# Four-image non-local block on one core: statistics, tile order of the last block, first exponentials, shared maxima and the final stage rebuilt

## The reference, cut to what matters

```
xn = group_norm(x, 32 groups)                      # per image
f = xn^T xn                                        # 4096 x 4096, symmetric
attn = softmax(f, axis=-1)
y = (g_w xn + g_b) attn^T                          # 128 x 4096
wy = W_w y + W_b                                   # 256 x 4096
wy = (wy - mean) * rsqrt(var + 1e-5) * gamma + beta  # over b, h, w
out = x + xn + wy
```

## Time and profile before

| | |
|---|---|
| median of 3 runs | 2142.32 us |
| the profiled execution's own time | 2144.3 us |
| its span | 2142.6 us |
| mean granted TensorE clock | 0.991 |
| busy: TensorE, VectorE, ScalarE, GpSimd | 96%, 73%, 51%, 38% |
| HBM read, written | 157.55 MB, 140.51 MB |

### The profile page before, as it was taken

One profiled execution on the slowest core, in us unless ns is written; L12 is line 12 of the kernel. 1 busy time (PEld: TensorE's weight loads), 2 busy tenths in 40 slices (PEclk: granted clock), 3 DMA queues, 4 the chain that ended last, 5 costly groups with the idle time before them and its releaser, 6 DMA issues.

```text
span 2142.6 us, 32272 instructions
## 1 busy us (share of the span) xinstructions
PE 2049.1 (96%) x9348; PEld 1459.3 (68%) x9348; DVE 1574.8 (73%) x3123; ACT 1086.5 (51%) x2234; POOL 810.9 (38%) x623
## 2 busy tenths in 40 slices
PE   5999999999999999999999999999999999999988
PEld 4787777656588777666668777765658777766433
DVE  5776777777776777787767677777777777777656
ACT  4344554455435445547454455445544554555645
POOL 4011233458501113448631123346850211345750
PEclk9999999999999999999999999999999999999999
DMA  3222233546412333455522223354641133347877
GB/s 125 116 96 87 94 117 113 191 142 201 157 66 74 114 120 107 164 176 156 185 88 97 88 94 117 113 191 142 200 158 77 58 118 113 99 133 235 306 284 294
DMA packets 107254, 300.29 MB, mean 140 GB/s; under 512 B 11456, under 2 KB 11840, under 8 KB 93248
## 3 DMA queue, kind: packets, MB, share of 16 engines
q1 hardware_dynamic: 107072, 298.11, 40.7%
HBM read 157.55 MB, written 140.51 MB: 139 GB/s over the span
## 4 chain that ended last, share of the span: by engine, by line
PE 76%; issue 7%; POOL 5%; DVE 5%; ACT 4%; DMA 2%; SPq 0%; DVEq 0%; ACTq 0%; POOLq 0%
PE bank L1258 14%; PE bank L1181 11%; PE bank L1183 11%; PE bank L1182 11%; PE bank L1234 8%; PE bank L1262 4%; PE bank L1264 4%; PE bank L1263 4%; PE bank L1411 2%; ACT ring L793 2%; POOL fy_c L726 2%; PE bank L1328 2%; POOL fy_d L726 2%; DMA fy_c<-spill 1%; DVE plo L1012 1%
## 5 line engine op out<-in xcount | busy, mean ns | idle before, releaser
L819 ACT CAST phi<-bank 128x512 fp32r<-128x512 f32 x480 | 282.2, 588 | 759.9 <-PE bank L1234 758.6
L976 DVE TENSOR_SCALAR_CACHE_REDUCE ring<-bank 128x512 f32<-128x512 f32 x560 | 385.6, 690 | 293.9 <-PE bank L1183 230.4
L1181 PE MATMUL bank<-xh 128*128 128x512 f32 (+3 forms) x1152 | 514.1, 446 | 6.1 <-POOL xl L699 5.9
L1012 DVE TENSOR_TENSOR plo<-bank,phi 128x512 fp32r<-128x512 f32 x480 | 329.2, 687 | 150.1 <-ACT phi L819 104.0
L1183 PE MATMUL bank<-xh,xl 128*128 128x512 f32 (+3 forms) x1152 | 436.1, 379 | 0.0
L1182 PE MATMUL bank<-xl,xh 128*128 128x512 f32 (+3 forms) x1152 | 433.7, 376 | 0.0
L793 ACT ACTIVATE ring<-ring,nmax 128x512 f32<-128x512 f32 x464 | 334.7, 723 | 37.0 <-DVE nmax L1003 37.0
L726 POOL TENSOR_TENSOR fy_d<-fy_d,maxrow 128x512 f32<-128x512 f32 x188 | 244.8, 1305 | 271.2 <-DMA fy_d<-spill 271.1
L1234 PEld LDWEIGHTS bank<-ident,ring 128*128 128x128 f32 x1856 | 223.5, 141 | 157.8 <-issue 84.7
L726 POOL TENSOR_TENSOR fy_c<-fy_c,maxrow 128x512 f32<-128x512 f32 x200 | 259.7, 1301 | 174.7 <-DMA fy_c<-spill 174.4
L1234 PE MATMUL bank<-ident,ring 128*128 128x128 f32 x1856 | 283.9, 276 | 21.6 <-DVE plo L1012 15.4
(11 more groups left out here) (138 smaller groups left out, 2770.5 us busy)
## 6 DMA issues: line engine op xcount, KB each, us to landing
spill<-ring SPq DMA_DIRECT2D x108, 1024.0 KB, 4.3
fy_c<-spill SPq DMA_DIRECT2D x200, 256.0 KB, 4.1
fy_d<-spill SPq DMA_DIRECT2D x188, 256.0 KB, 4.1
ring<-x_dram SPq DMA_DIRECT2D x42, 512.0 KB, 4.8
lbuf<-spill SPq DMA_DIRECT2D x60, 256.0 KB, 3.6
yd<-yn SPq DMA_DIRECT2D x24, 256.0 KB, 2.9
out_dram<-ring SPq DMA_DIRECT2D x10, 512.0 KB, 3.6
fx_a<-x_dram SPq DMA_DIRECT2D x8, 512.0 KB, 6.6
```

What stands on the lines that cost most here:

```text
L819: nc.scalar.copy(phi[:, HI_BUF[n], :], whole(p)).then_inc(hi_made, 1)
L976: last = nc.vector.tensor_scalar(slot_tile(u, t), src, 1.0, None, ALU.mult, ALU.max, accum_out=rowm[:, t, c:c + 1])
L1012: nc.vector.tensor_tensor(plo[:, n % LOS, :], whole(p), phi[:, HI_BUF[n], :].bitcast(F32), ALU.subtract).then_inc(lo_made, 1)
L1181: nc.tensor.matmul(dst, xh[:, k, rows], xh[:, k, cols], start=(k == 0), stop=False)
```

## The change

1. **Statistics**: STATS_STEP goes from 148, 149, 150, 151, 157, 164, 166, 167 to 142, 144, 149, 152, 157, 159, 165, 169; the group stages from 170, 172, 174, 175 to 172, 174, 176, 177; the normalization of x 2 steps later; the next image's first products at steps 184 to 238 (182 to 239 before).
2. **Block 7**: right, then 28 left, then 3 right tiles. Before: R R L R L R, then left tiles to the end.
3. **First exponentials**: chunk 0 of block 0 at steps -12, -11, -9, -8 (-7 to -4 before), chunk 1 at -3, -3, -2, -1, the last at step 20 (24 before).
4. **Maxima shared**: of the last image's blocks 6 and 7, 15 of 56 left tiles (every third from the fifth loaded one on, VSUBS) get their maxima subtracted by VectorE (`subtract_row`), 5 steps ahead of their step; GpSimd skips them.
5. **Final loads**: spread up to step 244. The first y goes from step 215 to 222; x of image 3 is loaded at 251 (piece 2) where before it was at 235 (piece 1).
6. **Final stage**: 30 half pieces (one k, 2 banks) and 4 quarter pieces in place of 16 pieces. The products of the first 4 (8 matmuls) are copied by ScalarE out of PSUM into `keep`, `lbuf`, `maxrow` and `lsb` ahead of `bn_ready`, and TensorE goes on with the next 4. `phi` and `plo` now lie where `keep` comes to lie later.

```diff
-    if j == NB - 1:
-        at = [0.04 * q for q in range(nr)]
-    elif j == NB - 2:
+    if j >= NB - 2:
         at = [0, 0.9, 0.95, 1]
...
-FIRST_EXP = -7
+FIRST_EXP = -12
...
+            if j == 0:
+                q = T * c + t
+                step = FIRST_EXP + 3 * q // 2 if q < T else (q - T) * 6 // 7 - 3
+            at[j, c, t] = max(step, min(merged, j * TPB - LAG - 1))
...
-STATS_STEP = [COLS_STEP[5] + 2 + c if c < 4 else X_STEP[c] + (12 if c == 5 else 6) for c in range(NB)]
+STATS_STEP = [X_STEP[c] + lag for c, lag in enumerate((6, 7, 9, 11, 6, 7, 5, 8))]
...
-NEXT_AT, NEXT_TO = XN_STEP[0] + 5, TILES - 17
+NEXT_AT, NEXT_TO = XN_STEP[0] + 5, TILES - 18
...
+VSUBS = [w for j in (NB - 2, NB - 1) for w in [w for w in LEFT_OF[j] if LEFT_BUF[w] is not None][VSUB_FROM::3]]
...
+UNITS = [(b, q, k, 0, FW // W) for b, q in PIECES[:-1] for k in range(K)] + \
+    [(*PIECES[-1], k, h, 1) for k in range(K) for h in range(FW // W)]
+KEPT = 4
...
+        def kept(u, h):
+
+            n = FW // W * u + h
+            if n < HIS + LOS:
+                return keep[:, n, :]
+            return (lbuf[:, 0, :], maxrow[:, :], lsb[:, :])[n - HIS - LOS]
...
+                    if not more and w in VSUBS:
+                        continue
...
                 w = LEFT_NO[p]
-                act.wait_ge(left_sub, b * NLEFT + w + 1)
+                if isinstance(b, int) and b == B - 1 and w in VSUBS:
+                    act.wait_ge(left_sub_v, VSUBS.index(w) + 1)
+                else:
+                    act.wait_ge(left_sub, pool_subs(b, w) + 1)
...
+            act.wait_ge(tile_used, B * TILES)
+            act.wait_ge(left_added, B * NLEFT)
+            for u in range(KEPT):
+                act.wait_ge(fin_wy, u + 1)
+                for h in range(FW // W):
+                    last = nc.scalar.copy(kept(u, h), unit_bank(u)[:, h, :])
+                last.then_inc(fin_kept, 1)
+
             act.wait_ge(bn_ready, 1)
...
+            def subtract_row(b, w):
+
+                mine = LOADS[LEFT_BUF[w]]
+                dve.wait_ge(loaded[LEFT_BUF[w]], b * (16 * len(mine)) + 16 * (mine.index(w) + 1))
+                dve.wait_ge(maxrow_made, b * (NB - 1) + tile(LEFT[w])[0])
+                nc.vector.tensor_tensor(left_at(w), left_at(w), maxrow[:, :], ALU.subtract).then_inc(left_sub_v, 1)
...
+                if not more and p + VSUB_LEAD in LEFT_NO and LEFT_NO[p + VSUB_LEAD] in VSUBS:
+                    subtract_row(b, LEFT_NO[p + VSUB_LEAD])
...
+                if u < KEPT:
+                    dve.wait_ge(fin_kept, u + 1)
+                    for a in range(n):
+                        last = nc.vector.scalar_tensor_tensor(out=px[:, a, :], in0=kept(u, a), scalar=bnp[:, 1, k:k + 1],
+                                                              in1=px[:, a, :], op0=ALU.mult, op1=ALU.add)
...
+                        elif u < 4 + KEPT:
+                            pe.wait_ge(fin_kept, u - 3)
                         else:
-                            pe.wait_ge(fin_added, f - 1)
+                            pe.wait_ge(fin_added, u - 3)
```

More of the change, by code:

```diff
@@ L245 @@
 X_STEP = [last_use(LAST_IN_SLOT[X_SLOT + c // 2]) + 1 + c % 2 for c in range(NB)]
-STATS_STEP = [COLS_STEP[5] + 2 + c if c < 4 else X_STEP[c] + (12 if c == 5 else 6) for c in range(NB)]
-assert all(s > X_STEP[c] + 5 for c, s in enumerate(STATS_STEP)) and STATS_STEP == sorted(STATS_STEP)
+STATS_STEP = [X_STEP[c] + lag for c, lag in enumerate((6, 7, 9, 11, 6, 7, 5, 8))]
+assert all(s >= X_STEP[c] + 5 for c, s in enumerate(STATS_STEP)) and STATS_STEP == sorted(STATS_STEP)
 GROUP_AT = STATS_STEP[-1] + 3
@@ L401, in nonlocal_block @@
             gl = scoped("gl", [P, NB, T, CI])
+            phi = scoped("phi", [P, HIS, W])
+            plo = scoped("plo", [P, LOS, W])
         fx_a = sb("fx_a", [P, K, N])
@@ L560, in left_at, with pool_subs, unit_bank, unit_x @@
             return (fy_c, fy_d)[h][:, row * W:(row + 1) * W]
+        def pool_subs(b, w):
+            n = b * NLEFT + w
+            return n - sum(v < w for v in VSUBS) if isinstance(b, int) and b == B - 1 else n
+        def kept(u, h):
[3 more added lines that the diff above has]
+            return (lbuf[:, 0, :], maxrow[:, :], lsb[:, :])[n - HIS - LOS]
+        def unit_bank(u):
+            return bank[:, 2 * (u % 4):2 * (u % 4) + UNITS[u][4], :]
+        def unit_x(u):
+            b, q, k, h, n = UNITS[u]
+            return fx(b, k, q)[:, h:h + n, :]
         def y_home(b, j):
@@ L677, in _ @@
                 load_final(False, 2, q)
[L678 to L685, removed]
-            sp.wait_ge(fin_out, 16 * K * B * FQ)
+            for q in range(FQ):
+                if LATE_X.get(q, TILES) >= TILES:
+                    load_final(True, 3, q)
+            for u, (b, q, k, h, n) in enumerate(UNITS):
+                cols = slice(q * FW + h * W, q * FW + (h + n) * W)
+                sp.wait_ge(fin_added, u + 1)
+                sp.dma_start(outd[b, :, k, cols].rearrange("p (a w) -> p a w", w=W), unit_x(u)).then_inc(fin_out, 16)
+            sp.wait_ge(fin_out, 16 * len(UNITS))
         @block.gpsimd
@@ L800, in take_maxrow @@
                 if j > 1:
-                    act.wait_ge(left_sub, b * NLEFT + LEFT_OF[j][0])
+                    act.wait_ge(left_sub, pool_subs(b, LEFT_OF[j][0]))
+                if isinstance(b, int) and b == B - 1 and VSUBS[0] < LEFT_OF[j][0]:
+                    act.wait_ge(left_sub_v, sum(v < LEFT_OF[j][0] for v in VSUBS))
                 nc.scalar.copy(maxrow[:, :], sps).then_inc(maxrow_made, 1)
@@ L1145, in _ @@
             last.then_inc(bn_ready, 1)
-            for f, (b, q) in enumerate(PIECES):
-                dve.wait_ge(fin_scaled, f + 1)
-                dve.wait_ge(fin_wy, f + 1)
-                for k in range(K):
-                    px = fx(b, k, q)
-                    wy = bank[:, 4 * (f % 2) + 2 * k:4 * (f % 2) + 2 * k + 2, :]
-                    last = nc.vector.scalar_tensor_tensor(out=px, in0=wy, scalar=bnp[:, 1, k:k + 1], in1=px,
+            for u, (b, q, k, h, n) in enumerate(UNITS):
+                dve.wait_ge(fin_scaled, u + 1)
+                px = unit_x(u)
+                if u < KEPT:
[3 more added lines that the diff above has]
+                                                              in1=px[:, a, :], op0=ALU.mult, op1=ALU.add)
+                else:
+                    dve.wait_ge(fin_wy, u + 1)
+                    last = nc.vector.scalar_tensor_tensor(out=px, in0=unit_bank(u), scalar=bnp[:, 1, k:k + 1], in1=px,
                                                           op0=ALU.mult, op1=ALU.add)
@@ L1423, in _ @@
             nc.tensor.matmul(lacc, wwt[:, P:2 * P], yn[:, :], start=True, stop=True).then_inc(wy_made, 1)
-            final_wy(0, [(1, 1)])
-            for f in range(1, len(PIECES)):
-                final_wy(f, [(0, 0), (0, 1), (1, 0), (1, 1)])
+            final_wy(1, [1])
+            for u in range(2, len(UNITS)):
+                final_wy(u, range(UNITS[u][4]))
 _INS = ("x", "wg", "bg", "ww", "vec")
```

77 lines of the change are left out of this document (44 added, 33 removed).

## The result

The changed kernel takes 2107.3 us (median of 4 runs, 2104.6 to 2111.0) against 2142.27: a ratio of 0.9835, interval 0.9818 to 0.9852. That is 35.0 us less where 29.7 were forecast, and inside the range. The profiled execution took 2108.62 us, with a span of 2106.9, so the two traces differ by 35.7 us of span.

A forecast was written before the change was run, and what follows sets the result against it. The prediction took TensorE, 76% of the chain, as the bound, with gains only where it waits or runs at half clock. Images 13.5, shared maxima 9.5 and final stage 6.7 sum to 29.7 us: 2112.6, range 2100 to 2125.

The forecast's parts named there:

- Statistics: Steps 148 to 150, images 0 to 2: shorter TensorE wait (1.24 us) and less half clock (1.5), gain 2.5 per image.
- Group stages: Steps 174 to 179: VectorE's lateness mostly moves to step 179, so only 0.5 of TensorE's 3.91 us wait is gained.
- Block 7 and first exponentials: Change of images: right tiles last and earlier exponentials shorten TensorE's 1.38 us wait and smaller gaps, 1.5 us per image.
- Shared maxima: Last image's blocks 6 and 7: 15 subtractions on VectorE, load pauses gone, right tiles charged; net gain 9.5 us.
- so the two fall in step and hardly wait: Blocks 6 and 7: per three tiles GpSimd needs 3.1 us and VectorE 3.0, instead of 3.75 on GpSimd.
- The lock: VectorE instructions with two SBUF inputs and GpSimd subtractions don't overlap; GpSimd's next is held back 0.45 to 0.6 us.
- the first rival: DMA becomes the bound in blocks 6 and 7; the last image gains 3 instead of 9.5 us, 2119; chance 0.17.
- The loads' 4.3: Blocks 6 and 7: first y at step 222 removes GpSimd's load pauses of 2.46 and 1.80 us, gaining 4.3.
- the right tiles' -4.3: Last image's block 7: three right tiles at the end have nothing to hide behind, costing 4.3 us.
- Final stage: After the last block: TensorE waits 1.6 us instead of 4.5 and the end comes earlier, gain 6.7 us.
- More than I count: Both stalls and their clock go, GpSimd has no pause left, final stage gives 7.5: 42 us, 2100; chance 0.14.
- "slower" rival: Blocks 6 and 7: VectorE gets its subtraction only after both of GpSimd's, 5.5 us per group, 2148; chance 0.04.

The follow-up runs named there:

- old_group: Changed kernel with the last statistic back at step 167 and the group stages at 170, 172, 174, 175, normalization and next products two steps sooner: 2116.84 us.
- no_shared: Changed kernel with all 56 maxima subtractions of the last image's blocks 6 and 7 back on GpSimd: 2110.80 us.
- old_block7: Changed kernel with block 7 in the old tile order, left tiles at the end: 2112.50 us.
- old_loads: Changed kernel with the final loads at their old steps (first y at 215), late pieces of x as new: 2109.27 us.
- free_all6: Changed kernel with left sums reduced into PSUM, only block 6's tiles shared, and gn_scale made by a tensor_scalar of one SBUF input: 2093.28 us.
- old_stats: Changed kernel with the statistics of x back at their old steps, except the last, which stays at 169: 2112.52 us.
- after_again: The changed kernel itself, unaltered, measured once more beside the kernel before: 2104.44 us, ratio 0.9831.

## Why the prediction was right, and where not

The total came out right by luck: its errors had both signs. Of the three terms the images gave 9.1 us more than forecast, blocks 5 to 7 of the last image 4.7 less, the final stage 1.7 more.

- **Statistics**: 2.5 us per image forecast, 2.82 in the blocks (58.09 to 55.27), 1.2 of it the wait and 1.6 the clock: 1.24 and 1.5 had been the terms. The last wait is 0.69, as worked out, and leaves the clock alone. The pairs at the new steps cost nothing visible. Right.
- **Group stages**: the failed step is "I take 0.5 of the 3.91 us as gain". The new wait in step 179 was named and is there, but is 1.40 us, not 3.4, and no half clock follows it. Undoing the step costs over 3 us per image. I charged VectorE's whole 2.6 us of lateness to the next left tile; the trace shows the wait behind an addition, after TensorE had other work. And I took VectorE's time as only moved, where the maxima got 1.4 us shorter (old_group). The clock, which stood in the bounds and not in the 0.5, was at 1.2 GHz for 3.4 us or more behind this wait in all three images of before and of old_group, and in none of the changed kernel.
- **Block 7 and first exponentials**: 1.5 forecast. The two undone singly cost 2.1 and 1.7 in image 0. Undersized; the upper bound of 3.4 was the better number.
- Together the images before the last image's block 5 gave 22.6 where the term said 13.5, though image 1 had lost 4.2 to the miss.
- **Shared maxima**: 9.5 forecast for blocks 6 and 7, 5.2 seen, and of this little by sharing (0.6 between the two traces, which is within their spread). The step that failed is "so the two fall in step and hardly wait". The lock is there as foreseen: the subtraction takes 1.31 us on average in block 6, GpSimd's next 1.7 where it follows at once (four of seven). But VectorE's side of the sum, "3 x 0.8 + 0.6 = 3.0", has only 0.6 for the subtraction, room for its own 0.69 or for the lock's wait and not for both. With the 1.31 measured 3.7 come out, against 3.57 from the trace and 3.75 before, and hardly a gain was to be expected. (The sum's "0.63" is itself 0.65, 3.75 less 3.1, which changes nothing.)

  In block 7 the first rival holds. What gained instead is the order of block 7: 2.9 by its undoing, 1.7 of it clock.

  The kernel before also lost there what the forecast had in its rows and did not price: the pause of 2.68 us that was to "stay" made TensorE wait 2.82 us, and the 0.96 of the earlier trace rows is 6.8 us at 1.2 GHz behind it. Neither is in the changed kernel or in no_shared, where block 7 takes 4.0 us less than before and block 6 0.6 less. The old order brings the stop back (old_block7), the old load steps alone do not (old_loads). How the rest divides among order and loads stays open. The loads' 4.3 and the right tiles' -4.3 cancelled in the sum and were both wrong.

  On DMA's rate had 407 GB/s over four us, and the changed kernel's final stage has 393 over twenty (last row below). The 358 of the Trainium skill ("DMA: Bandwidth & Descriptors", "Where 436 GB/s comes from") is under both. In the 19 us of block 6 the rate was 354 at a share of 0.98, so a share near 1 goes with rates from 354 to 407 here.
- **Final stage**: 6.7 forecast, 8.4 measured. Timeline of the changed kernel's final stage, and a window of it:

```profile
2055.00 3.40 DVE L1224 SCALAR_TENSOR_TENSOR fx_a<-keep,bnp,fx_a 128x512 f32<-128x512 f32 x5 [1.72 <-ACT fx_a L966]
...
2061.64 8.85 PE L1492 MATMUL bank<-ring,wwt 128*128 128x512 f32 x20 [2.06 <-DVE fx_a L1228]
...
2099.78 4.18 DVE L1228 SCALAR_TENSOR_TENSOR gf<-bank,bnp,gf 128x1024 f32<-128x1024 f32 x5 [0.43 <-PE bank L1492]
```

```profile
2062.00:2082.00 20.00, 20.00 (x48) 8.83 (x47) 16.82 (x14) 20.00 (x18) 0.00 (x0) 1.00 0.98 393
```

  TensorE goes on 17.3 us after block 7's inverse (forecast 17.2: 2088.9 less 2071.68), having waited 2.06 (forecast 1.6). From there to the end of the last addition, at 2103.96, are 42.3 us (forecast 42.6). These terms gave 6.9 for 6.7. The other 1.5 is the last store, which now ends 2.9 us after the last addition instead of 4.4; it was named as a bound and not counted.
- **The rivals**: DMA as bound holds for block 7, and begins at the end of block 6. "More than I count" holds for the images, not for the blocks it named. The "slower" rival's mechanism exists: L1114 and L1087, not L1098, fell to it, with 6.4 us or more 8 times in 13 traces, at 4.2 to 5.3 us each in the two blocks concerned.

## To carry to other kernels

- Before tuning, list VectorE's instructions that take SBUF inputs only, and look in the trace for those that last as long as GpSimd's neighbour. Giving one of them a PSUM input moved as much time here (11.6 us) as the largest single part of the change (10.9, by undoing the group stages).
- Work given from a slower engine to a faster one must be priced with its own time and with what both do to each other, and the next supplier (here the loads) must have room; else the wait only changes its name.
- Look at the granted clock in every window where TensorE waits, and price it. About half of this gain was clock, and the forecast's sum priced it in one place of three.
- If runs of one kernel lie in steps, profile until one of the longer ones is caught, and compare it block by block. The medians of 4 to 6 such runs did not settle effects of 3 us here.

## What the runs showed of the hardware

- A VectorE instruction that needs SBUF beside GpSimd's is let in at a border of two subtractions, or misses it. For block 6 of images 0 to 2, L1114 started 1.00 to 1.09 us into one of 1.3 in 24 places of the traces: it ended in 0.25 to 0.31 us in 18 of them, in 6.43 to 6.47 in six. A miss lasted not for one more instruction but until GpSimd itself had to wait for a load: five more subtractions passed in these six, four in the two of L1087 (6.60 and 6.64), one in two others (2.43 and 2.58 us).
- Two SBUF inputs are not needed for it: a TENSOR_SCALAR from SBUF to SBUF (free_all6) took 1.23, while the TENSOR_REDUCE that makes `lsum` and the RECIPROCAL that makes `linv`, both on SBUF alone, never took over 0.18 (32 each in the changed kernel, 24 and 23 of them beside a GpSimd instruction).
- The same wait of TensorE is or isn't followed by 3.4 us at 1.2 GHz. After 1.92 us they came in three of three places in the kernel before, and in one of three in old_stats; after 3.24 us (L1395) they didn't come in the changed kernel, after 3.26 they did in after_again. I can't tell from the traces what decides it.
